# A mixture-of-experts layer behind windowed attention: shared tiles ahead of the expert search, deviations for two pairs at once, routed sums behind the low part

## The chip, the cores and the metric

The kernel runs on one core of one Trainium2 chip. Its time is the device time of one execution in microseconds (us); three runs were taken. The engines are PE (TensorE), DVE (VectorE), ACT (ScalarE), POOL (GpSimd) and SP (SyncE, here a DMA queue).

## The reference, cut to what matters

`x` has 4 x 2048 tokens of 256 channels (8192 tokens, 64 tiles of 128). The layer is two residual steps:

```python
x = x + layernorm(attn(layernorm(x), w_lin))
y = layernorm(x)
x = x + layernorm(ffn(y))

def ffn(y):
    shared = silu(y @ shared_w_gate.T) * (y @ shared_w_up.T) @ shared_w_down.T   # 704 inner columns
    shared = shared * sigmoid(y @ shared_gate_w.T)
    probs = softmax(y @ gate_w.T)                       # 16 experts
    rw, sel = top_k(probs, 2); rw = rw / rw.sum(-1)
    routed = sum over the two chosen experts: rw * (silu(g) * h) @ w_down[e],  g, h = split(y @ w_gate_up[e])
    return routed + shared
```

All products are made of three float32r products (a number is split in a high part, which is what float32r holds of it, and a low part, which is the rest), so every operand of a product is first copied to its high part (by ACT) and then subtracted to its low part (by DVE).

## The kernel before, in words

There are three stages behind the attention stage, which ends at about 391 us. The order of the work of each engine is written out by hand, with semaphores between the engines.

**Shared tiles.** The 8192 tokens are 16 tiles `n` of 512; each is worked in 6 steps `m` over the 704 inner columns (five of 128, a last one of 64). `Shared.products` is PE's order: in each step it makes the gate and up products of two steps ahead (`gate_up`, L788, 12 matmuls; 6 in the last step of a tile), then what `between` puts in, then `down` of this step (L804, 12 matmuls; 8 in the last). ACT makes silu (`silu`, L746) and the high part of the inner product (`inner_high`, L751), DVE the gated product `hf` (`gated`, L768) and its low part (`inner_low`, L774: tile `hl`, in a last step `hh`). PE's `gate_up` of step k+2 waits for `hf` of step k, `down` of step k waits for its low part. ACT's `leave` takes a whole tile's result out of PSUM.

**Routing stage** (`route_and_share`, tiles 0 to 6: 42 steps, k = 6 n + m). DVE first finds the two best experts of the last 8 token tiles (`choose`, which calls `top.find`) and marks both choices for all 64 tiles (`chosen`), and then begins the 42 steps. Behind `inner_low` of its step stands a part of the routing: weights (k = 0), counts (1), bases (2), `before` (3), places (4), slots (5, 6), rows and blocks (6), block columns (7). From step `LIST_FROM` = 8 on, over 26 steps, DVE writes a group of five list entries (`listed`, L1066 and L1067), POOL their other operand (`in_row`, L945), and PE sums them one step later (`take`, L1131, five matmuls). The finished list gives the row numbers of each expert block (`ids`, step 35); POOL gathers the first four blocks with them. Expert weights are loaded on SP's queue, copied by ACT (`COPY_AT`) and lowered by DVE (`LOW_AT`) between the steps. ACT's exponents of the routing (`gap`, `zs`) need the Exp table; they stand ahead of step 0, between two loads of tables. `done` makes DVE wait for its own operation.

**Expert stage** (`experts`): 144 blocks of 128 rows; POOL gathers their rows (L843), the result goes to `expert_rows` in DRAM.

**Closing stage** (`shared_and_combine`, tiles 7 to 15: 54 steps). Beside the shared tiles it finishes all tokens in 32 units of two tiles of 128 tokens. `sums_at` says in which step DVE makes the `sums` of a unit. For each unit POOL gathers four times 128 expert rows (`gather`, L1380, tile `cy`), DVE adds both routed rows, weighted, to the shared result `ff`, and takes mean and variance (`sums`, L1438 to L1450; eight operations), POOL makes one over the deviation (`scales`, L1387 an add, L1389 a power with exponent -0.5), ACT centres `ff` one step behind the sums (`centred`, L1402), and DVE multiplies and adds `x` (`finish`, L1486), `finish_at` = four steps behind the sums. SP stores the unit. POOL's queue is `scales` of a unit, then the gathers of four units later (`AHEAD` = 4). The last two units need the last tile of the shared part: `routed_sums` (L1457, L1461) prepare them in steps 3 and 4 of tile 15, ahead of DVE's next gated product; `last_sums` (L1471 to L1478) add the shared part when PE is done, and `finish` of the last two ends the kernel. In between, units 28 and 29 are finished ahead of `last_sums`.

Of the kernel before, what the change touches and what calls it, by code (L numbers as in the profile page):

```python
# [12 lines left out]
ALU = mybir.AluOpType  # L13
ACT = mybir.ActivationFunctionType
# [696 lines left out]
CHUNKS = T // 512  # L711
# [135 lines left out]
GROUP = 5  # L847
LISTS = NT * TOPK
GROUPS = -(-LISTS // GROUP)
LIST_FROM = 8  # L850
COPY_AT = {4 + 2 * e: e for e in range(13)} | {36: 13, 38: 14, 40: 15}
LOW_AT = {5 + 2 * e: e for e in range(13)} | {37: 13, 39: 14, 41: 15}
LOAD_AT = {2 * e: e for e in range(15)} | {38: 15}
# [2 lines left out]
def route_and_share(nc, block, sh, sems, we, split, parts, eh, el, xg, xg_in, turned, ynt_d, yn_d, logits, slots, share, shgate, ids,  # L856
# [4 lines left out]
    with ExitStack() as ctx:  # L861
# [88 lines left out]

        @block.scalar
        def _(act):
            act.preload_act_table(ACT.Exp)
            nc.scalar.activation(ones_r[:], ones[:], ACT.Copy)
            act.wait_ge(s["below_ok"], 2)
            nc.scalar.activation(below_r[:], below[:], ACT.Copy).then_inc(s["below_ok"], 1)
            act.wait_ge(s["gap_ok"], 1)
            nc.scalar.activation(gap[:], gap[:], ACT.Exp).then_inc(s["exp_ok"], 1)
            nc.scalar.activation(zs[:], logits[:, :, E], ACT.Exp, scale=-1.0).then_inc(s["exp_ok"], 1)
            act.preload_act_table(ACT.Silu)  # L960

            def leave(n):
                if n > 0:
                    act.wait_ge(s_kept, n * 16)
                sh.leave(act, n, lambda t: (so[:, t:t + 1], s["so_ok"]))

            for n in range(FIRST):
                for m in range(FT):
                    k = n * FT + m
                    sh.silu(act, n, m)  # L970
                    if m == 1 and n > 0:
                        leave(n - 1)
                    sh.inner_high(act, n, m)
                    if m == 2:
                        sh.split_high(act, n + 1)
                    if k in COPY_AT:
                        e = COPY_AT[k]
                        act.wait_ge(s[f"e_in{e % 2}"], e // 2 * 16 + 16)
                        nc.scalar.activation(eh[:, e:e + 1], eraw[:, e % 2:e % 2 + 1], ACT.Copy).then_inc(s["e_hi"], 1)
# [6 lines left out]
        def _(ve):  # L986
# [5 lines left out]
            def choose():  # L992
                top.find(ve, top.EARLY, NT, pick, rest)
                v.tensor_tensor(gap[:], best[:, 1], best[:, 0], ALU.subtract).then_inc(s["gap_ok"], 1)
# [79 lines left out]
                v.tensor_tensor(el[:, e:e + 1], eraw[:, e % 2:e % 2 + 1], eh[:, e:e + 1].bitcast(F32),  # L1074
                                ALU.subtract).then_inc(s["e_lo"], 1)

            choose()
            chosen()
            for n in range(FIRST):
                for m in range(FT):  # L1080
                    k = n * FT + m
                    sh.gated(ve, n, m)
                    if m == 3:
                        sh.split_low(ve, n + 1)
                    if k in LOW_AT and k > 34:
                        expert_low(LOW_AT[k])
                    if k == LIST_FROM + GROUPS + 1:
                        ve.wait_ge(s["taken_ok"], GROUPS)
                        done(v.tensor_copy(ids_f[:], pb[6][:, NBK:2 * NBK]))
                        v.scalar_tensor_tensor(ids[:], pb[6][:, 0:NBK], float(P), ids_f[:], ALU.mult, ALU.add  # L1090
                                               ).then_inc(s["ids_ok"], 1)
                    sh.inner_low(ve, n, m)
                    if k == 0:
                        weights()
                    if k == 1:
                        counts()
                    if k == 2:
                        bases()
                    if k == 3:
                        before()  # L1100
                    if k == 4:
                        places()
                    if k == 5:
                        slots_of(0)
                    if k == 6:
                        slots_of(1)
                        rows_and_blocks()
                    if k == 7:
                        block_columns()
                    if k == 11:  # L1110
                        ve.wait_ge(s["turn_ok"], 1)
                        done(v.tensor_copy(block_expert[:, 0:NBK], pb[7][0:1, 0:NBK]))
                    if k in LOW_AT and k < 34:
                        expert_low(LOW_AT[k])
                    if 0 <= k - LIST_FROM < GROUPS:
                        listed(k - LIST_FROM)

        @block.tensor
        def _(pe):
            hb = both[:].rearrange("p t e -> p (t e)")  # L1120

            def sums(of):
                for k in range(2):
                    nc.tensor.matmul(pb[6 + k][:], of[:], hb[:, 512 * k:512 * k + 512], start=True, stop=True).then_inc(s["sums_ok"], 1)

            def take(g):
                pe.wait_ge(s["listed_ok"], g + 1)
                pe.wait_ge(s["rowed_ok"], g + 1)
                for j in range(g * GROUP, min(g * GROUP + GROUP, LISTS)):
                    w = j % (2 * GROUP)  # L1130
                    ins = nc.tensor.matmul(pb[6][:, 0:2 * NBK], in_row[:, w], in_blk[:, w].rearrange("p v w -> p (v w)"),  # L1131
                                           start=(j == 0), stop=(j == LISTS - 1), skip_group_check=True)
                ins.then_inc(s["taken_ok"], 1)

            def between(n, m):
                k = n * FT + m
                if k == 0:
                    pe.wait_ge(s["below_ok"], 3)
                    pe.wait_ge(s["both_ok"], 1)
                    sums(ones_r)  # L1140
                if k == 2:
                    pe.wait_ge(s["cs_ok"], 1)
                    sums(below_r)
                if k == 9:
                    pe.wait_ge(s["bcol_ok"], 1)
                    for c in range(NBT):
                        ins = nc.tensor.matmul(pb[7][0:1, c * P:(c + 1) * P], bcol[:, c:c + 1], ident[:], start=True, stop=True)
                    ins.then_inc(s["turn_ok"], 1)
                if 0 <= k - LIST_FROM - 1 < GROUPS:
                    take(k - LIST_FROM - 1)  # L1150
                if m == 0 and n > 0:
                    pe.wait_ge(s["so_ok"], n * 4)
                if k == FIRST * FT - 1:
                    pe.sem_inc(x_full, 8)
                    pe.wait_ge(sems["hf_ok"], FIRST * FT - 1)
                    for b in range(2):
                        pe.wait_ge(xg_in[b], 16)
                        for c in range(CC):
                            ins = nc.tensor.transpose(pb[b][:, c * P:(c + 1) * P], xg[:, b, c * P:(c + 1) * P], ident[:])
                        ins.then_inc(x_full, 1)  # L1160
            sh.products(pe, 0, FIRST, between)
# [152 lines left out]
def shared_and_combine(nc, block, sh, yo_out, sems, split, turned, ynt_d, x2_d, yg_d, s_kept, sh_d, neg_half, eps, slots, share, shgate, out, pb):  # L1314
# [13 lines left out]
    UNITS = len(order)  # L1328
    place = {unit: i for i, unit in enumerate(order)}
    steps = [(n, m) for n in range(FIRST, CHUNKS) for m in range(FT)]  # L1330
    finish_at = {steps[k + 4]: sums_at[at] for k, at in enumerate(steps) if at in sums_at and k + 4 < len(steps)}
    centre_at = {steps[k + 1]: sums_at[at] for k, at in enumerate(steps) if at in sums_at and k + 1 < len(steps)}
    with ExitStack() as ctx:
        def sb(name, shape, dt=F32):
# [35 lines left out]
        def _(po):  # L1370
# [12 lines left out]

            def scales(i):
                r = i % R
                po.wait_ge(s["mv_ok"], i * 2 + 2)
                nc.gpsimd.tensor_tensor(rstd[:, r], mv[:, r, :, 1], eps[:, 0:2], ALU.add).then_inc(s["var_ok"], 1)  # L1387
                po.wait_ge(s["var_ok"], i + 1)
                nc.gpsimd.tensor_tensor(rstd[:, r], rstd[:, r], neg_half[:, 0:2], ALU.pow).then_inc(s["dev_ok"], 1)  # L1389
            for i in range(UNITS + AHEAD):  # L1390
                if i >= AHEAD:
                    scales(i - AHEAD)
                if i < UNITS:
                    gather(i)

        @block.scalar
        def _(act):
# [30 lines left out]
        def _(ve):  # L1428
# [60 lines left out]
            for n in range(FIRST, CHUNKS):  # L1489
                for m in range(FT):  # L1490
                    sh.gated(ve, n, m)
                    if m == 1 and n + 1 < CHUNKS:
                        sh.split_low(ve, n + 1)
                    if (n, m) in finish_at:
                        finish(finish_at[n, m])
                    if (n, m) in sums_at:
                        sums(sums_at[n, m])
                    if (n, m) == (FIRST, 0):
                        for k in range(8):
                            ve.wait_ge(yo_out[k], 16 + NBK // 8 * 16)  # L1500
                    sh.inner_low(ve, n, m)
                    if n == CHUNKS - 1 and m in (3, 4):
                        routed_sums(UNITS - 2 + m - 3)
            for i in range(UNITS - 2):
                if i not in finish_at.values():
                    finish(i)
            for i in (UNITS - 2, UNITS - 1):
                last_sums(i)
            for i in (UNITS - 2, UNITS - 1):
                finish(i)  # L1510

# [36 lines left out]
```

## Time and profile before

| | |
|---|---|
| three runs | 1035.18, 1038.87, 1041.07 us (median 1038.87) |
| the profiled execution | 1037.57 us, span of its core 1035.8 us |
| busy | PE 92%, DVE 82%, POOL 56%, ACT 53% of the span |
| instructions | 26916 |

The span is the profiled execution from its first to its last instruction; the execution's own time is 1.8 us longer. PE's load of weights runs beside its matmuls. "issue" is time in which an engine waited for nothing that the profile shows; a releaser is inferred from semaphores. DMA issues on POOL count as its busy time where the row says DMA_INDIRECT.

### The profile page before, as it was taken

The numbers are of one execution on the slowest core, as the hardware profiler recorded it, in microseconds if no ns is written. First come the engines' busy times: TensorE is split into PE (matmuls) and PEld (weight loads), VectorE is DVE, ScalarE is ACT, GpSimd is POOL, SyncE is SP. The second block draws the span as 40 slices with busy tenths as digits, with TensorE's granted clock in tenths as the row PEclk, the third lists the DMA queues.
The fourth block names the chain that finished last, engine by engine and source line by source line (L and its number), as shares of the span: only waits on it lengthen the run. The fifth ranks groups of instructions, "written<-read, shape, count | busy, mean of one in ns | idle before, by whom it ended". The sixth has DMA issues, their size and how long they took to land.

```text
span 1035.8 us, 26916 instructions
## 1 busy us (share of the span) xinstructions
PE 951.2 (92%) x9256; PEld 833.6 (80%) x9256; DVE 844.7 (82%) x2278; ACT 550.8 (53%) x1308; POOL 582.2 (56%) x843
## 2 busy tenths in 40 slices
PE   5997899899789976899999999999999999999994
PEld 4766788687678865788888899999999878788883
DVE  5887998789799868888886588888888678788886
ACT  4995354799434453333434555555555445454542
POOL 4441655622056540268884366666662688888874
PEclk9998999899999988999999999999999999999996
DMA  5532578843268851122232465555556656665653
GB/s 164 172 110 59 163 208 247 259 124 113 65 173 225 236 186 62 50 88 62 76 119 62 88 202 176 179 177 175 176 180 134 188 178 186 190 199 172 207 166 110
DMA packets 155811, 158.17 MB, mean 153 GB/s; under 512 B 52528, under 2 KB 135600, under 8 KB 155696
## 3 DMA queue, kind: packets, MB, share of 16 engines
q1 hardware_dynamic: 137648, 113.98, 35.7%
q0 software_dynamic: 13056, 35.67, 13.0%
q10 hardware_dynamic: 4992, 6.95, 2.2%
q8 instruction: 78, 1.28, 0.5%
q14 instruction: 37, 0.30, 0.1%
HBM read 91.90 MB, written 64.63 MB: 151 GB/s over the span
## 4 chain that ended last, share of the span: by engine, by line
PE 25%; POOL 17%; DVE 12%; issue 4%; ACT 2%; DMA 1%; POOLq 0%; DVEq 0%; SPq 0%; ACTq 0%
POOL cy L1380 14%; PE bank L1245 11%; PE bank L1261 5%; PE bank L788 3%; PE bank L1230 3%; DVE in_blk L1067 2%; POOL crstd L1389 2%; PE bank L804 2%; DVE in_blk L1066 2%; DVE hf L768 2%; DVE hl L774 2%; ACT hh L751 1%; PE bank L1254 1%; DVE el L1074 1%; POOL crstd L1387 1%
## 5 line engine op out<-in xcount | busy, mean ns | idle before, releaser
L843 POOL DMA_INDIRECT xg<-yn_scratch,ids x144 | 137.0, 951 | 94.2 <-PE bank L1230 65.3
L1380 POOL DMA_INDIRECT cy<-expert_rows,slots x128 | 143.4, 1120 | 56.4 <-issue 36.5
L751 ACT ACTIVATE hh<-hf 128x512 fp32r<-128x512 f32 x96 | 60.7, 633 | 202.9 <-DVE hf L768 202.9
L788 PE MATMUL bank<-yh,gh 128*128 128x512 f32 x352 | 141.0, 401 | 12.5 <-DVE hf L768 12.3
L667 PE MATMUL bank<-xbd,am 128*32 128x68 f32 x4096 | 138.3, 304 | 13.6 <-DMA xbd<-xn_scratch 7.9
L667 PEld LDWEIGHTS bank<-xbd,am 128*32 128x32 f32 x4096 | 123.0, 129 | 21.3 <-issue 10.4
L788 PE MATMUL bank<-yh,gl 128*128 128x512 f32 x352 | 140.1, 398 | 0.0
L788 PE MATMUL bank<-yl,gh 128*128 128x512 f32 x352 | 139.2, 395 | 0.0
L945 POOL TENSOR_SCALAR in_row<-col,row_f 128x128 bf16<-128x128 bf16 x128 | 96.6, 771 | 65.6 <-DVE row_f L1051 39.6
L804 PE MATMUL bank<-dh,hh 128*128 128x256 f32 x384 | 110.2, 292 | 11.8 <-DVE hl L774 8.0
L804 PE MATMUL bank<-dl,hh 128*128 128x256 f32 x384 | 106.5, 282 | 0.0
L1245 PE MATMUL bank<-eh,xh 128*128 x288 | 100.4, 348 | 1.6 <-issue 0.6
L804 PE MATMUL bank<-dh,hl 128*128 128x256 f32 x320 | 90.8, 284 | 0.0
L804 PEld LDWEIGHTS bank<-dh,hh 128*128 128x128 f32 x384 | 73.3, 191 | 18.7 <-DVE hl L774 11.0
L788 PEld LDWEIGHTS bank<-yh,gh 128*128 128x128 f32 x352 | 66.8, 190 | 26.0 <-DVE hf L768 12.2
L356 POOL TENSOR_TENSOR rstd<-mv,eps 128x2 f32<-128x2 f32 (+1 forms) x68 | 14.1, 208 | 129.1 <-DVE mv L440 82.5
L450 DVE TENSOR_TENSOR am<-probs,mask 128x512 f32<-128x512 f32 x128 | 80.0, 687 | 8.2 <-ACT probs L545 7.2
L768 DVE TENSOR_TENSOR hf<-sg,bank 128x512 f32<-128x512 f32 x96 | 65.5, 682 | 24.1 <-ACT sg L746 23.2
L382 POOL TENSOR_TENSOR x<-av,xr 128x256 f32<-128x256 f32 x64 | 47.0, 754 | 65.9 <-ACT yn L568 62.5
L1245 PE MATMUL bank<-el,xh 128*128 x288 | 81.2, 282 | 0.0
L1245 PE MATMUL bank<-eh,xl 128*128 x288 | 80.7, 280 | 0.0
L788 PEld LDWEIGHTS bank<-yh,gl 128*128 128x128 f32 x352 | 66.7, 189 | 15.6
(184 smaller groups left out, 2684.2 us busy)
## 6 DMA issues: line engine op xcount, KB each, us to landing
expert_rows<-yo SPq DMA_DIRECT2D x144, 128.0 KB
xbd<-xn_scratch SPq DMA_DIRECT2D x128, 72.0 KB, 2.3
xt<-xp SPq DMA_DIRECT2D x32, 256.0 KB, 2.7
xn_scratch<-xn SPq DMA_DIRECT2D x64, 128.0 KB, 2.7
xr<-x SPq DMA_DIRECT2D x32, 256.0 KB, 3.6
x_scratch<-x SPq DMA_DIRECT2D x32, 256.0 KB, 3.8
yn_scratch<-yn SPq DMA_DIRECT2D x32, 256.0 KB, 3.7
ynt_scratch<-ynt SPq DMA_DIRECT2D x32, 256.0 KB, 4.4
```

Source lines behind the costliest of these rows:

```text
L382: nc.gpsimd.tensor_tensor(x2[:, q, t], av[:, q, t], xr[:, q, t], ALU.add).then_inc(s["x2_ok"], 1)
L450: nc.vector.tensor_tensor(am[:, q, g], probs[:, bass.ds(i * CB, CB), g, None, :].to_broadcast([P, CB, 2, J]), mask[:, None].to_broadcast([ ...
L667: ins = nc.tensor.matmul(pso[q][t][J * b:J * b + J, g * MW:(g + 1) * MW], am[:, q, g, e, side], xbd[:, q, e + side, :, g], start=(g == 0 a ...
L751: self.nc.scalar.activation(self.hh[0:f, g], self.hf[0:f, k], ACT.Copy).then_inc(self.s["hh_ok"], 1)
L768: self.nc.vector.tensor_tensor(self.hf[0:f, k], self.sg[0:f, k], up, ALU.mult).then_inc(self.s["hf_ok"], 1)
L788: ins = self.nc.tensor.matmul(self.pb[2 * k + half][:], w[:, c, col:col + P], y[:, n % 2, c, :], start=(j == 0), stop=(j == 5))
L804: ins = self.nc.tensor.matmul(o, a[:, g, t * P:(t + 1) * P], w[:, m, :], start=(m == 0 and t % 2 == 0 and j == 0), stop=(m == FT - 1 and j ...
L843: return nc.gpsimd.indirect_dma_start(out=to, out_offset=None, in_=yn_d.rearrange("n p c -> (n p) c"), in_offset=bass.IndirectOffsetOnAxis ...
L945: ins = nc.gpsimd.tensor_scalar(in_row[:, w], col[:, 0:P], row_f[:, k, t:t + 1], None, ALU.is_equal)
L1245: ins = nc.tensor.matmul(pg[r % 2][:, 0:2 * MF], a[:, r % 2, c * P:(c + 1) * P], w[:, bass.ds(e, 1), c * C:(c + 1) * C], start=(j == 0), s ...
L1261: ins = nc.tensor.matmul(py[r % 2][:, 0:C], a[:, r % 2], w[:, bass.ds(e, 1), 2 * C:3 * C], start=(j == 0), stop=(j == 2))
L1380: nc.gpsimd.indirect_dma_start(out=y[:, r, t, j], out_offset=None, in_=yg_d, in_offset=bass.IndirectOffsetOnAxis(ap=slots[:, 2 * unit + t, ...
```

## The change

Four edits, all of order and grouping; what is computed stays the same.

1. Routing stage: DVE begins with step 0 of the shared tiles; `choose` stands behind it, `chosen` behind step 1, and the other parts one to three steps later than before. ACT begins with the Silu table; the exponents, between loads of Exp and of Silu, stand in step 3. PE's sums and the turned columns come two steps later.
2. The list is written and taken in steps 10 to 35 instead of 8 to 33; `ids` come in step 37.
3. Closing stage: POOL's `scales` work on two units with one add and one power of four columns, and its loop handles two units: `scales` of a pair, then eight gathers. A unit is finished six steps behind its sums (even) or five (odd).
4. `routed_sums` move from steps 3 and 4 of the last tile to steps 4 and 5, and units 28 and 29 are finished behind `last_sums`.

```diff
-LIST_FROM = 8
+LIST_FROM = 10
...
         @block.scalar
-            act.preload_act_table(ACT.Exp)
+            act.preload_act_table(ACT.Silu)
...
-            act.wait_ge(s["gap_ok"], 1)
-            nc.scalar.activation(gap[:], gap[:], ACT.Exp).then_inc(s["exp_ok"], 1)
-            nc.scalar.activation(zs[:], logits[:, :, E], ACT.Exp, scale=-1.0).then_inc(s["exp_ok"], 1)
-            act.preload_act_table(ACT.Silu)
+            def exponents():
+                act.preload_act_table(ACT.Exp)
+                act.wait_ge(s["gap_ok"], 1)
+                nc.scalar.activation(gap[:], gap[:], ACT.Exp).then_inc(s["exp_ok"], 1)
+                nc.scalar.activation(zs[:], logits[:, :, E], ACT.Exp, scale=-1.0).then_inc(s["exp_ok"], 1)
+                act.preload_act_table(ACT.Silu)
...
                     sh.inner_high(act, n, m)
+                    if k == 3:
+                        exponents()
...
-            choose()
-            chosen()
             for n in range(FIRST):
...
                     sh.inner_low(ve, n, m)
                     if k == 0:
+                        choose()
+                    if k == 1:
+                        chosen()
+                    if k == 3:
+                        counts()
+                    if k == 4:
+                        bases()
                         weights()
-                    if k == 1:
-                        counts()
-                    if k == 2:
-                        bases()
-                    if k == 3:
+                    if k == 5:
                         before()
-                    if k == 4:
+                    if k == 6:
                         places()
-                    if k == 5:
+                    if k == 7:
                         slots_of(0)
-                    if k == 6:
+                    if k == 8:
                         slots_of(1)
+                    if k == 9:
                         rows_and_blocks()
-                    if k == 7:
                         block_columns()
-                    if k == 11:
+                    if k == 13:
...
-                if k == 0:
+                if k == 2:
                     pe.wait_ge(s["below_ok"], 3)
                     pe.wait_ge(s["both_ok"], 1)
                     sums(ones_r)
-                if k == 2:
+                if k == 4:
                     pe.wait_ge(s["cs_ok"], 1)
                     sums(below_r)
-                if k == 9:
+                if k == 11:
...
-    finish_at = {steps[k + 4]: sums_at[at] for k, at in enumerate(steps) if at in sums_at and k + 4 < len(steps)}
+    behind = {at: k + (6 if sums_at[at] % 2 == 0 else 5) for k, at in enumerate(steps) if at in sums_at}
+    finish_at = {steps[k]: [sums_at[at] for at in behind if behind[at] == k] for k in behind.values() if k < len(steps)}
+    finished = [i for units in finish_at.values() for i in units]
...
-                po.wait_ge(s["mv_ok"], i * 2 + 2)
-                nc.gpsimd.tensor_tensor(rstd[:, r], mv[:, r, :, 1], eps[:, 0:2], ALU.add).then_inc(s["var_ok"], 1)
-                po.wait_ge(s["var_ok"], i + 1)
-                nc.gpsimd.tensor_tensor(rstd[:, r], rstd[:, r], neg_half[:, 0:2], ALU.pow).then_inc(s["dev_ok"], 1)
-            for i in range(UNITS + AHEAD):
+                po.wait_ge(s["mv_ok"], i * 2 + 4)
+                nc.gpsimd.tensor_tensor(rstd[:, r:r + 2], mv[:, r:r + 2, :, 1], eps[:].rearrange("p (a b) -> p a b", a=2), ALU.add
+                                        ).then_inc(s["var_ok"], 1)
+                po.wait_ge(s["var_ok"], i // 2 + 1)
+                nc.gpsimd.tensor_tensor(rstd[:, r:r + 2], rstd[:, r:r + 2], neg_half[:].rearrange("p (a b) -> p a b", a=2), ALU.pow
+                                        ).then_inc(s["dev_ok"], 2)
+            for i in range(0, UNITS + AHEAD, 2):
                 if i >= AHEAD:
                     scales(i - AHEAD)
                 if i < UNITS:
                     gather(i)
+                    gather(i + 1)
...
-                    if n == CHUNKS - 1 and m in (3, 4):
-                        routed_sums(UNITS - 2 + m - 3)
-            for i in range(UNITS - 2):
-                if i not in finish_at.values():
-                    finish(i)
+                    if n == CHUNKS - 1 and m in (4, 5):
+                        routed_sums(UNITS - 2 + m - 4)
             for i in (UNITS - 2, UNITS - 1):
                 last_sums(i)
+            for i in range(UNITS - 2):
+                if i not in finished:
+                    finish(i)
             for i in (UNITS - 2, UNITS - 1):
                 finish(i)
```

## Rows read from the trace of the kernel before

**Rows 1.** The page's first part: busy time, share of the span, instructions.

```profile
PE 951.2 (92%) x9256; PEld 833.6 (80%) x9256; DVE 844.7 (82%) x2278; ACT 550.8 (53%) x1308; POOL 582.2 (56%) x843
```

**Rows 2.** Busy time by windows: stretch, length, each engine's busy time (instructions), PE clock, DMA.

```profile
804.00:1020.00 216.00, 208.04 (x1183) 179.69 (x1182) 175.38 (x414) 105.61 (x207) 174.26 (x186) 1.00 0.61 184
1020.00:1036.00 16.00, 3.94 (x18) 3.35 (x16) 9.54 (x26) 2.44 (x5) 3.54 (x7) 0.50 0.26 85
```

**Rows 3.** Waits, 803 to 1036: who <- for whom, us in total, times, longest.

```profile
POOL cy L1380 <- issue: 36.5, 127, 1.2
...
DVE cx L1486 <- issue: 14.6, 11, 3.2
...
PE bank L804 <- DVE hl L774: 8.0, 5, 2.7
...
DVE cff L1457 <- DMA cy<-expert_rows,slots: 3.5, 2, 2.5
```

**Rows 4.** Timeline, closing stage: start, us, what, [idle before it <- releaser].

```profile
806.32 0.94 POOL L1380 DMA_INDIRECT cy<-expert_rows,slots  x1 [19.91 <-DMA expert_rows<-yo]
...
828.27 0.21 POOL L1387 TENSOR_TENSOR crstd<-cmv,eps 128x2 f32<-128x2 f32 x1
...
884.31 0.72 POOL L1389 TENSOR_TENSOR crstd<-crstd,neg_half 128x2 f32<-128x2 f32 x1
...
885.11 0.88 DVE L1486 SCALAR_TENSOR_TENSOR cx<-cff,crstd,cx 128x256 f32<-128x256 f32 x2 [3.18 <-issue]
...
1018.62 0.95 POOL L1380 DMA_INDIRECT cy<-expert_rows,slots  x1 [0.30 <-issue]
```

**Rows 5.** Groups of POOL by shape, whole span: count | busy us, mean ns | idle.

```profile
L1380 POOL DMA_INDIRECT cy<-expert_rows,slots x128 | 143.4, 1120 | 56.4 <-issue 36.5 <-DMA expert_rows<-yo 19.9
...
L359 POOL TENSOR_TENSOR rstd<-rstd,neg_half 128x4 f32<-128x4 f32 x28 | 28.5, 1017 | 2.2
L359 POOL TENSOR_TENSOR rstd<-rstd,neg_half 128x2 f32<-128x2 f32 x40 | 28.4, 711 | 3.1
L1389 POOL TENSOR_TENSOR crstd<-crstd,neg_half 128x2 f32<-128x2 f32 x32 | 23.9, 746 | 2.5
...
L1387 POOL TENSOR_TENSOR crstd<-cmv,eps 128x2 f32<-128x2 f32 x32 | 10.5, 329 | 9.2 <-DVE cmv L1478 8.5
```

**Rows 6.** Timelines of DVE and PE, end of the closing stage.

```profile
1001.78 0.29 DVE L1450 BATCH_NORM_AGGREGATE cmv<-cst 128x2 f32<-128x6 f32 x2
...
1021.82 0.62 DVE L1457 TENSOR_SCALAR cff<-cy,share 128x256 f32<-128x256 f32 x2 [2.48 <-DMA cy<-expert_rows,slots]
...
1030.82 0.88 DVE L1486 SCALAR_TENSOR_TENSOR cx<-cff,crstd,cx 128x256 f32<-128x256 f32 x2
1032.35 0.88 DVE L1486 SCALAR_TENSOR_TENSOR cx<-cff,crstd,cx 128x256 f32<-128x256 f32 x2 [0.64 <-POOL crstd L1389]
...
1019.40 0.39 PE L804 MATMUL bank<-dh,hh 128*128 128x256 f32 x1 [2.66 <-DVE hl L774]
...
1025.38 0.58 PE L804 MATMUL bank<-dh,hh 128*128 128x256 f32 x1 [3.52 <-DVE hh L774]
...
1027.04 0.41 PE L804 MATMUL bank<-dl,hh 128*128 128x256 f32 x1
```

**Rows 7.** Timelines of the routing stage's beginning.

```profile
395.26 1.28 ACT L960 ACT_TABLE_LOAD   x1
396.56 0.60 ACT L746 ACTIVATE sg<-bank 128x512 f32<-128x512 f32 x1
...
399.06 0.79 PE L788 MATMUL bank<-yh,gh 128*128 128x512 f32 x1 [8.10 <-DVE hf L768]
...
438.22 0.37 DVE L1066 TENSOR_SCALAR in_blk<-col,blk_f 128x144 bf16<-128x144 bf16 x1
...
440.36 0.67 DVE L768 TENSOR_TENSOR hf<-sg,bank 128x512 f32<-128x512 f32 x1
...
449.25 0.79 PE L1131 MATMUL bank<-in_blk,in_row 128*128 128x288 bf16 x5
...
455.10 0.67 DVE L768 TENSOR_TENSOR hf<-sg,bank 128x512 f32<-128x512 f32 x1
```

More of the change, by code:

```diff
@@ L1493, in _ @@
                         sh.split_low(ve, n + 1)
-                    if (n, m) in finish_at:
-                        finish(finish_at[n, m])
+                    for i in finish_at.get((n, m), ()):
+                        finish(i)
                     if (n, m) in sums_at:
@@ L1501, in _ @@
                     sh.inner_low(ve, n, m)
-                    if n == CHUNKS - 1 and m in (3, 4):
-                        routed_sums(UNITS - 2 + m - 3)
-            for i in range(UNITS - 2):
-                if i not in finish_at.values():
-                    finish(i)
+                    if n == CHUNKS - 1 and m in (4, 5):
+                        routed_sums(UNITS - 2 + m - 4)
             for i in (UNITS - 2, UNITS - 1):
                 last_sums(i)
+            for i in range(UNITS - 2):
+                if i not in finished:
+                    finish(i)
             for i in (UNITS - 2, UNITS - 1):
```

## The prediction

> **What bounds the kernel now.** I read the page first, then busy time by windows, the waits of each stage, and last the timelines around the edits. The page says PE is busy 92% of the span and POOL 56% [rows 1]. That mean hides three stages: routing (391 to 584 us), experts (584 to 804), closing (804 to the end). The edits touch the first and the last.
>
> In the closing stage PE is busy 208 of 216 us up to 1020, and then 3.94 of 16 us at half the full clock, the lower of its two levels (1.2 GHz) [rows 2]. So PE is the bound there, and what can be won is its idle time. The waits name it: 8.0 us waiting for the low part hl of DVE and 3.5 us for the last low part (hh), 11.5 us in all [rows 3, 6]. DVE is late because it waits itself: 14.6 us ahead of the finishing operation (L1486) and 3.5 us ahead of the routed sums (L1457) for gathered rows [rows 3]. The first is printed as "issue", but a timeline shows what it is: POOL's power for that unit starts at 884.31 and runs 0.72, to 885.03; DVE had been idle 3.18 and starts at 885.11 [rows 4]. Both waits go back to POOL, which from 806.32 to 1019.57 issues without a rest [rows 4]: 32 units, 6.66 us each, hardly faster than PE uses them up. POOL's pace is the hidden bound.
>
> In the routing stage PE sits idle 8.10 us until DVE has found the last top two and marked them, and starts at 399.06 [rows 7]. After that DVE is nearly saturated until the list is written.
>
> **The change, part by part.**
>
> *Deviations for two units at once.* A unit costs POOL four gathers and one block (add, power). A gather is 1.12 busy [rows 5]; with the pause behind it, about 1.425 (the tile's issues have 36.5 us of such pauses [rows 3]): 128 of them are 182.4 us, and 28 blocks of 1.065 (0.329 + 0.746, [rows 5], small pauses, less the pause saved at a gather) are 29.8, together 212.2 against 213.25 measured [rows 4], so these are the right sizes. A doubled block works on four columns instead of two. The attention stage has both widths of the same power: 1.017 us against 0.711 [rows 5], so 0.31 more; the add does not grow. A pair then costs 1.375 instead of 2.13: 0.755 less, and 14 pairs stand ahead of the last gather: 10.6 us less work on POOL.
>
> The edit adds a wait: a block, and the eight gathers queued behind it on POOL, wait for the sums of the pair's second unit, and DVE's next sums wait for those gathers. At the end of the stage this cap binds: the last eight gathers stand behind the sums of unit 27, which end at 1002.07 today [rows 6] and, with the 5.3 us of PE's idle time ahead of it gone (11.5 - 2.66 - 3.52), near 997. Then 1.4 for the block and 8 times 1.425: issue ends at 1009.6, landing 2.2 later (today the last issue ends at 1019.57 and DVE starts at 1021.82, [rows 4, 6]), so 1012. If nothing of the 5.3 goes, 1017.
>
> *Finishing five or six steps behind the sums instead of four.* Between a unit's sums and its finishing now lie at least 20 us instead of 17, while the deviation comes earlier. I take all 14.6 us of DVE's idle time there as gone. Its price: at six of the steps two units are finished at once (0.8 each, two operations as in [rows 6]) between the gated product and the low part. Five of these have sums as well (2.5: two each of four operations, the last of them in [rows 6]): 0.6 + 1.6 + 2.5 + 0.6 = 5.3 us of DVE. A full step of PE takes 4.2 (the 54 steps, some of them shorter, take 1027.5 - 804 less 11.5 and 1.8: 3.9 each). But these five stand between lighter ones, and a low part is due only 2.8 us after its gated product; so nothing, at most 1.1 us each, 5.5.
>
> *Routed sums behind the low part.* Today these two stand ahead of DVE's next gated product while gathers are awaited: PE idles 2.66 before 1019.40 and 3.52 before 1025.38 [rows 6]. Moved one step back, the first stands after PE has all it needs of its step, and the second has nothing of PE behind it. What is late next is the last low part itself: DVE does routed sums (1.33), the gated product, two finishings (1.6) and the low part (0.6), and PE waits some 2.5 us for it. So of 11.5 us idle 2.5 stay. Today's idle also brought the lower clock: the two last groups took 2.27 and 1.9 instead of 1.42 and 0.95 (the last matmul shows 0.41, against 0.28 where the clock is full), 1.8 us; I take that as gone. The last product ends at 1027.45 today [rows 6]: 1027.45 - 9.0 - 1.8 = 1016.7.
>
> *The tail.* Last sums run from there to 1030.82, and DVE ends at 1032.35 + 0.88 = 1033.23 [rows 6]; the span ends 2.6 later, with the store. Now finishing of units 28 and 29 stands behind the last sums (before, it filled the wait for PE), and the deviations of the last two come together. Last sums 3.3, then four finishings 3.3; the paired block (0.38 + 0.08 + 0.82 + 0.31 = 1.6) lies beside the first two. DVE ends at 1016.7 + 6.6 + 0.1 = 1023.4, which is 9.8 earlier. Four stores leave within 3.3 us instead of two: 0.3 more. **Closing stage: 9.5 us gained.** Bounds: 7 less gain if the cap binds (1.5 to 2) and every crowded step costs; 2.5 more if the last wait goes too.
>
> *Shared tiles ahead of the search, list over ten steps.* PE's idle 8.10 falls to about 3.4: a table load from 391.24, two small copies and silu (1.28 + 0.5 + 0.6, [rows 7] for the first and last) give DVE its first product near 393.7 instead of 398.3. But DVE then stands still 2.4 us waiting for that silu, and its work is the same. It has no slack to give: I followed its order and found it the last to be ready at nearly every step up to the list. Today it begins step 12 at 455.10 [rows 7], having written four lists, of 440.36 - 438.22 = 2.14 each. Now two lists (4.28) and one small copy (0.33) come later, and 2.4 plus 0.8 (a silu that stands behind the splitting of the next tile) are lost idle: 455.10 - 4.6 + 3.2 = 453.7. PE begins that step about 1.0 to 1.4 earlier, with two more list products still to do (five matmuls each, begun at 449.25 and shown as 0.79 long [rows 7]; 0.53 until the next product begins). From there both engines run at about 4.6 us per step in either kernel, and the waits at tile changes come out a little larger. Net: +0.3 us, so the 4.7 us that PE starts earlier come back as waits of 0.5 to 2 us for DVE through the steps 2 to 10. PE's restart at the lower clock (3 us of it) is the same in both. Bounds: 2 us gained, if DVE's order leaves more slack than I see; 3 lost.
>
> *Exponents in step 3.* ACT does a table load, two small operations and a load: 1.30 + 0.57 + 1.30 = 3.2 us ahead of the silu of step 4. DVE counts in that time (3.8), so it costs nothing; 1.1 us of cover is left. The row is clear: the load takes 1.28 us and the next operation begins 0.02 behind it [rows 7]. The Trainium skill (ScalarE: Activation LUTs, What ACT_TABLE_LOAD costs) adds a drain of about 1.38 us to each switch, 2.66 in all. By that rule the block would be 5.9 us and the sum 1.7 worse; the trace does not agree, and the row is used.
>
> *List two steps later.* The ids come at step 37, not 35, some 9 us later; the four gathers behind them on POOL are needed in step 41 and were 15 us early. The low part of expert 13 waits for the last list product, which moves it by some 4.5 us; SP's load for expert 15 waits for that, and its copy in step 40 keeps 4 us of slack. Nothing.
>
> **Sum.** -9.5 + 0.3 = -9.2 us. The profiled execution took 1037.57 (span 1035.8), 1.3 below the median 1038.87 of the three runs, which spread over 6 us. From one base 1028.4, from the other 1029.7; I say 1029.0.
>
> **Rivals.**
> (A) Half a gain: the pair wait and the crowded steps take over the place of the waits removed. For it: the cap is real. Against: 3 us of room in front of it. Price: last gathers at 1017 instead of 1012 (2.2 late for the routed sums), 3.3 for three of the five crowded steps, routing +1: gain 3, time about 1035.5.
>
> (B) POOL's gathers stretch. The steady pitch of 1.425 is itself a guess for a denser stage. If it rose by 0.1, the whole 10.6 us would be used up, and every 0.01 beyond that adds 1.28 us, since all 128 are in line. At 1.58, 11% more, the kernel ends 5 to 6 us later than before: about 1044. It decides from 1.53 on. For it: the first sixteen, with less work on DVE beside them, come at (828.27 - 806.32) / 16 = 1.37 [rows 4], the mean is 1.425. Against: those sixteen have no block between them, so gathers need no block to recover in. The Trainium skill (GPSIMD Engine Reference, Specifications) says GpSimd shares its way into SBUF with VectorE, contended by instructions with two SBUF inputs; these are the finishing and sums. DVE's share would go from 81 to some 85%, and by that rule pitch rises slightly; no row isolates it.
>
> (C) The change in the routing stage wins after all: PE keeps 3 of its 4.7 us. Then 1026. Against: DVE has no free time.
>
> (D) The routed sums alone matter and POOL's pace was no bound: gain 3.2, 1035.
>
> **Chances.** Forecast (1024 to 1032) 0.58, C 0.10, A and D together 0.22, B 0.10 (half of it beyond the bound of a change). A measurement of this kernel can tell 0.5%, 5.2 us. Faster by more: 0.75; within: 0.19; slower: 0.06. Range 1023.5 to 1036: from forecast and C's side to A and D; the forecast's own is 1024 to 1032.
>
> **What would show it.** Right: no DVE idle ahead of L1486 but at the very end; POOL's blocks half as many, with a power of about 1.0; last gather issue ended by 1013; PE's idle time in the closing stage at 2 to 4 us, nearly all before the last low product; in the routing stage PE restarting near 394.4, and the stage still ending within 2 us of 584. Wrong: gathers longer than 1.2 us on average; POOL waiting for sums all along the stage; PE idle ahead of the steps with two finishings; a routing stage shorter or longer by over 3 us.

## The result, and the profile after

The changed kernel takes 1030.31 us (median of 19 runs, 1027.1 to 1035.99), the kernel before beside it 1039.76 (19 runs). The ratio is 0.9906, interval 0.9893 to 0.9920: 9.4 us faster. 1029.0 was predicted. One run of e2 (1468.91 us) and one of e4 (1155.79 us) had a mean granted clock of 0.56 and 0.74 and stand in no ratio below.

The page after, busy time by engine [rows 1]:

```profile
PE 949.1 (92%) x9256; PEld 833.5 (81%) x9256; DVE 844.5 (82%) x2278; ACT 552.4 (54%) x1309; POOL 567.4 (55%) x811
```

The shares hardly move; only POOL's 32 fewer instructions show. By windows of the stages (columns as in [rows 2]):

```profile
806.00:1013.00 207.00, 207.00 (x1183) 180.74 (x1182) 171.71 (x408) 105.23 (x206) 158.72 (x155) 1.00 0.62 190
1013.00:1029.00 16.00, 4.13 (x29) 3.63 (x27) 12.70 (x35) 3.35 (x8) 4.12 (x6) 0.66 0.42 138
```

In the closing stage PE is now busy without a gap up to 1013, where it had 8 us of gaps in 216. The waits that were there before the last tile (5.3 us in all) are gone, so the steps with two finishings cost PE nothing. The waits of DVE there, 803 to 1029 [rows 3]:

```profile
DVE cff L1449 <- DMA cx<-x_scratch: 1.9, 2, 1.3
DVE cff L1449 <- DMA cy<-expert_rows,slots: 1.7, 1, 1.7
...
DVE cx L1497 <- issue: 0.2, 1, 0.2
```

The 14.6 us ahead of the finishing are 0.2, and the 3.5 ahead of the routed sums are gone. New is a wait for `cx<-x_scratch`, the load of `x` (and with it of the shared result) for a unit. POOL, at its first block and at its last gather [rows 4]:

```profile
833.78 1.05 POOL L1398 TENSOR_TENSOR crstd<-crstd,neg_half 128x4 f32<-128x4 f32 x1
...
1013.76 0.96 POOL L1388 DMA_INDIRECT cy<-expert_rows,slots  x1 [0.30 <-issue]
```

It issues from 811.14 to 1014.72, 203.6 us for what took 213.25, 9.7 less. The groups [rows 5] and, below them, the end on DVE and PE [rows 6]:

```profile
L1388 POOL DMA_INDIRECT cy<-expert_rows,slots x128 | 139.7, 1091 | 58.3 <-issue 36.7 <-DMA expert_rows<-yo 20.3 <-DVE cff L1454 1.2
...
L1398 POOL TENSOR_TENSOR crstd<-crstd,neg_half 128x4 f32<-128x4 f32 x16 | 18.9, 1178 | 2.6 <-POOL crstd L1395 0.4
```

```profile
1017.75 0.39 PE L804 MATMUL bank<-dh,hh 128*128 128x256 f32 x1 [2.37 <-DVE hh L774]
...
1019.08 0.41 PE L804 MATMUL bank<-dl,hh 128*128 128x256 f32 x1
...
1022.86 1.67 DVE L1497 SCALAR_TENSOR_TENSOR cx<-cff,crstd,cx 128x256 f32<-128x256 f32 x4
1024.69 1.67 DVE L1497 SCALAR_TENSOR_TENSOR cx<-cff,crstd,cx 128x256 f32<-128x256 f32 x4 [0.17 <-issue]
```

One idle time of PE is left, 2.37 us ahead of the last products, which need the last low part. In the routing stage [rows 7]:

```profile
395.23 0.50 PE L788 MATMUL bank<-yh,gh 128*128 128x512 f32 x1 [3.35 <-DVE hf L768]
...
446.41 0.47 PE L788 MATMUL bank<-yh,gh 128*128 128x512 f32 x1 [2.13 <-DVE hf L768]
```

PE restarts 4.75 us earlier, counted from attention's end (390.96 before, 391.88 here), and at 446.41 0.9 are left of it.

All stage lengths below (us) are read from one profile each, the ratios from all runs of the kernel. Routing is from the end of attention's last matmul to the first turned expert rows. Closing is from its first matmul to DVE's end. PE idle is what PE waits for DVE in the closing stage.

| kernel | ratio to before, interval | routing | closing | PE idle |
|---|---|---|---|---|
| before | 1 | 191.6 | 231.4 | 11.5 |
| changed | 0.9906, 0.9893 to 0.9920 | 193.3 | 220.3 | 2.4 |
| e1_closing | 0.9908, 0.9882 to 0.9933 | 193.0 | 219.9 | 2.4 |
| e2_routing | 0.9995, 0.9976 to 1.0014 | 193.1 | 231.1 | 12.2 |
| e3_pairs | 0.9924, 0.9896 to 0.9952 | 191.9 | 221.8 | 3.7 |
| e4_tail | 0.9962, 0.9943 to 0.9982 | 191.7 | 226.8 | 6.4 |
| e5_finish | 0.9975, 0.9949 to 1.0001 | 191.8 | 228.8 | 10.8 |
| e6_pairs_tail | 0.9901, 0.9867 to 0.9935 | 191.7 | 219.3 | 1.5 |
| e7_no_pairs | 0.9944, 0.9918 to 0.9970 | 192.4 | 224.3 | 3.0 |
| e8_extra_power | 0.9976, 0.9948 to 1.0004 | 193.1 | 228.3 | 5.8 |
| e9_late_share | one run, 1027.82 us | 191.1 | 219.9 | 2.4 |
| e10_pairs_tail_late | 0.9892, 0.9870 to 0.9914 | 191.7 | 219.3 | 1.5 |
| e11_one_input | one run, 1023.44 us | 192.2 | 218.6 | 2.8 |

### The profile page after: what moved, and what is told of

Read it like the earlier page. It is cut to its first block, busy times and chain, and to the rows that moved or that the text cites. A ratio compares the mean times of both kernels' runs of the same rounds, so it can differ in the third digit from the quotient of the medians.

```text
span 1029.0 us, 26902 instructions
## 1 busy us (share of the span) xinstructions
PE 949.1 (92%) x9256; PEld 833.5 (81%) x9256; DVE 844.5 (82%) x2278; ACT 552.4 (54%) x1309; POOL 567.4 (55%) x811
## 4 chain that ended last, share of the span: by engine, by line
PE 35%; DVE 19%; ACT 4%; issue 2%; DMA 1%; SPq 0%; DVEq 0%; POOL 0%; POOLq 0%; ACTq 0%
PE bank L1251 11%; PE bank L788 10%; PE bank L804 5%; PE bank L1267 5%; DVE hf L768 3%; PE bank L1236 3%; DVE hl L774 2%; DVE in_blk L1072 2%; ACT hh L751 2%; DVE in_blk L1071 2%; PE bank L1260 1%; DVE cff L1449 1%; DVE cx L1497 1%; DVE cff L1454 1%; DVE el L1079 1%
## 5 line engine op out<-in xcount | busy, mean ns | idle before, releaser
L1388 POOL DMA_INDIRECT cy<-expert_rows,slots x128 | 139.7, 1091 | 58.3 <-issue 36.7
L667 PEld LDWEIGHTS bank<-xbd,am 128*32 128x32 f32 x4096 | 122.8, 129 | 21.9 <-issue 10.6
L1280 ACT ACTIVATE xh<-bank 128x256 fp32r<-128x256 f32 x144 | 55.3, 385 | 43.7 <-PE bank L1236 42.6
```

The source lines that it names most:

```text
L667: ins = nc.tensor.matmul(pso[q][t][J * b:J * b + J, g * MW:(g + 1) * MW], am[:, q, g, e, side], xbd[:, q, e + side, :, g], start=(g == 0 a ...
L1280: nc.scalar.activation(xh[:, r % 2], px[r % 2][:, 0:C], ACT.Copy).then_inc(s["xh_ok"], 1)
L1388: nc.gpsimd.indirect_dma_start(out=y[:, r, t, j], out_offset=None, in_=yg_d, in_offset=bass.IndirectOffsetOnAxis(ap=slots[:, 2 * unit + t, ...
```

## The experiments

**Which half.** e1 has `route_and_share` of before and `shared_and_combine` of the changed kernel, e2 the reverse.

> The routing stage of before with the closing stage of the changed kernel (deviations in pairs, finishing five or six steps behind, routed sums behind the low part). Theory (POOL's pace and the tail were the whole gain, the routing edit gives nothing or takes 1 to 2 us): 9.5 to 11 us faster than before, ratio 0.990 or a little under, PE idle in the closing stage 2 to 4 us. Rival (both halves gain): 5 to 7 us faster only, the rest in the routing stage.

> The routing stage of the changed kernel with the closing stage of before. Theory: the routing stage, counted from its first to its last matmul, is 1 to 2 us longer than before (the profile of the changed kernel showed 1.6), so the whole is the same or 1 to 2 us slower, ratio 1.000 to 1.002. Rival (the earlier start of PE is kept): 3 to 4 us faster, ratio 0.997.

Measured: e1 is as fast as the changed kernel, e2 as before. The closing stage holds the whole gain; e2's interval leaves room for 2.5 us gained or 1.5 lost. The same order gave routing lengths that differ by 1.3 us from trace to trace, so e1's 193.0 says little by itself. Over all traces above, before's order of that stage (before, e1, e3 to e6, e11) has a mean of 192.0, the changed order (changed, e2, e7, e8) 193.0. By these traces it costs about 1.0 us; the two groups overlap only in e1, and the times can't tell so little.

**Which of the three closing edits.** e3 keeps the pairs alone, e4 the end alone, e5 the finishing alone, e6 the pairs and the end. Against the changed kernel, cut to what matters:

```diff
 # e3, e4, e6: finishing as before
-    behind = {at: k + (6 if sums_at[at] % 2 == 0 else 5) ...}
+    behind = {at: k + 4 ...}
 # e3, e5: end as before; units 28 and 29 are finished ahead of last_sums
-                    if n == CHUNKS - 1 and m in (4, 5):
+                    if n == CHUNKS - 1 and m in (3, 4):
 # e4, e5: scales(i) of one unit and a POOL loop over single units, as before
```

> Before with the paired deviations alone: finishing stays four steps behind, routed sums and the last finishings stay where they were. Theory (POOL's pace is the bound of the closing stage): 6 to 8 us faster, ratio 0.993; DVE's idle time ahead of the finishing falls from 16 to some 4 us; PE idle in the stage about 5 us instead of 11.5. Rival (the order at the end is what matters): 0 to 2 us faster.

> Before with the last routed sums one step later, behind the low part, and units 28 and 29 finished behind the last sums; deviations unit by unit. Theory: 3 us faster (2 to 4), since one of the two long waits ahead of the last low parts goes and POOL's last gathers still end at the same time; ratio 0.997. Rival (this edit is the gain): 7 us or more faster.

> Before with the finishing of a unit five or six steps behind its sums instead of four, and nothing else. Theory (POOL's pace is the bound): DVE's idle time ahead of the finishing goes from 16 to some 1 us, yet the time stays within 1.5 us of before, since DVE then waits for gathered rows at its next sums. Rival (the wait of the finishing is itself what costs): 4 to 5 us faster.

> Before with paired deviations and the new order at the end; finishing four steps behind as before. Theory: 8.5 to 9.5 us faster, all but 1 us of the closing stage's gain: the later finishing adds at most 1 us once POOL is fast. Rival (the three edits add up): 3 us or more less than the whole.

Measured in the closing stage: pairs 9.6 us, end 4.6, finishing 2.6; pairs and end together 12.1, all three 11.2 and 11.6 (changed, e1). They overlap: each takes some of the same waits. e3's time came out where expected (7.9 us, 0.9924), its stage 2 us better. By their ratios e4 gained 4.0 us (2 to 4 expected) and e6 10.3 (8.5 to 9.5 expected). e5 gained 2.6, more than the 1.5 that were allowed, with an interval that touches 1. Its trace shows the idle time move, as expected:

```profile
DVE cff L1440 <- DMA cy<-expert_rows,slots: 6.0, 5, 3.5
...
DVE cff L1459 <- DMA cy<-expert_rows,slots: 3.7, 2, 2.7
DVE cff L1440 <- DMA cx<-x_scratch: 1.4, 1, 1.4
DVE cx L1488 <- POOL crstd L1391: 0.6, 1, 0.6
```

The 16.4 us ahead of the finishing are 0.9, and 9.7 stand ahead of the gathered rows instead of 5.0. e6 shows that the later finishing is not needed: without it the stage is 0.6 to 1.0 us shorter, by one trace of it and two with it.

**POOL's time or the grouping.** e7 is the changed kernel with `scales` and POOL's loop of before. e8 is the changed kernel with one more power per pair:

```diff
+                nc.gpsimd.tensor_tensor(extra[:, i // 2]..., mv[:, r:r + 2, :, 1], neg_half[:]..., ALU.pow)
                 po.wait_ge(s["var_ok"], i // 2 + 1)
```

> The changed kernel with the deviations taken back to one unit at a time (two gathers' groups apart), all else as changed. POOL's work ahead of its last gather grows by 10.6 us. Theory: 6 to 8 us slower than the changed kernel, that is 2 to 4 us faster than before; the last gather's issue ends as late as before, counted from the stage's start. Rival (the pairing did nothing): as fast as the changed kernel.

> The changed kernel with one more power of four columns per pair on POOL, written to a tile that nobody reads: 1.1 to 1.2 us more for each of 14 pairs ahead of the last gather, 16 us in all, of which the first 3 or 4 fall into POOL's free time. Theory: the whole gain of the change is given back, 10 to 14 us slower than the changed kernel and 0 to 4 us slower than before. Rival (the doubling matters for its grouping, not for POOL's time): within 2 us of the changed kernel.

Measured: e7's closing stage is 4.0 us longer than the changed kernel's, e8's 8.0 (by the ratios about 4 and 7; e7's interval just touches the changed kernel's, e8's does not). Direction and order are those of the theory: POOL's time is what counts, with the grouping in place or not. DVE waits for gathered rows again ahead of the routed sums, in e7 for 3.2 us (the row below) and in e8 for 3.5:

```profile
DVE cff L1465 <- DMA cy<-expert_rows,slots: 3.2, 1, 3.2
```

The sizes missed the bounds: 6 to 8 and 10 to 14 were expected, and the issue of e7's last gather ends 212.8 us into the stage, where before it was 217.8 and "as late as before" was expected. The groups of e7 and e8 say why in part:

```profile
L1388 POOL DMA_INDIRECT cy<-expert_rows,slots x128 | 136.8, 1069 | 55.3 <-issue 35.6 <-DMA expert_rows<-yo 19.8
```

```profile
L1389 POOL DMA_INDIRECT cy<-expert_rows,slots x128 | 136.1, 1063 | 56.9 <-issue 36.7 <-DMA expert_rows<-yo 19.9 <-DVE cff L1457 0.3
L1398 POOL TENSOR_TENSOR extra<-cmv,neg_half 128x4 f32<-128x4 f32 x16 | 20.1, 1254 | 0.0
```

A gather is not a constant: 1.12 us before, 1.09 changed, 1.07 and 1.06 here, which over 128 gathers is 2.9 us less in e7 than in the changed kernel and 3.6 in e8. The rest is idle time of POOL that its longer blocks fill. From its first gather to its last, the blocks of e7 take 32.9 us against 20.5 in the changed kernel, 12.4 more, but the 2.9 us for which the changed kernel's POOL waits for the pair's sums are gone, and so are 2.1 us of other pauses. That leaves 4.5 us.

**Is it DVE's reading?** e11 is before with the two additions of routed rows and the finishing made of operations that read one tile; it leaves out what its expectation names. The first of the three:

```diff
-scalar_tensor_tensor(ff[:, r, t], y[:, r, t, 0], share[:, k:k + 1, 0], ff[:, r, t], ALU.mult, ALU.add)
+tensor_scalar(ff[:, r, t], y[:, r, t, 0], share[:, k, 0:1], None, ALU.mult)
```

> Before, with three kinds of DVE operation of the closing stage (both additions of routed rows, the finishing) reading one SBUF tile instead of two; left out by this are the shared part, the first routed row and the residual of all units but the last two's sums. Theory (gathers on POOL stretch while DVE reads two SBUF tiles): the mean gather falls from 1.12 us to 1.05 or less, and POOL ends its last gather 7 us or more earlier, counted from its first. Rival (gathers stretch by themselves, by the DMA queue): mean stays within 0.03 of 1.12.

Measured: mean 1.057, just over the bound set of 1.05; POOL's issue ends 202.2 us after its first gather, 11 earlier. But e3 and e5 to e8, whose operations read two tiles, have 1.06 to 1.08, so this does not tell reading two tiles from reading at other moments. It is inconclusive on the cause: the gathers' length moves with DVE's work beside them, and by what part of it stays open. The stage is shorter too, 218.6, but DVE's own work in it fell from 185 to 166 us by the same edit, so this says nothing of POOL.

**Who paces the routing stage.** e9 is the changed kernel with `shares()` (three of the five operations of `weights`) behind step 38; e10 has e6's closing stage and the same move in before's order.

```diff
+                    if k == 38:
+                        shares()
```

> The changed kernel with half of the weights of the routing (three DVE operations, 0.98 us, which only the closing stage reads) moved from step 4 to step 38. Theory (DVE sets the routing stage up to the end of the list in the changed order): that stage, from the last product of attention to the first turned expert rows, is about 1 us shorter than the changed kernel's 192.4 to 193.3. Rival (PE is the bound there and DVE's load does not count): unchanged.

> Before's routing order with the share of the weights moved to step 38, paired deviations, the new order at the end, and finishing four steps behind as before. Theory: closing stage 219 to 220 us from its first matmul to DVE's end, routing stage about 191.7, so 10 to 11 us faster than before and 1 to 2 us faster than the changed kernel, ratio 0.989 to 0.990. Rival (the changed kernel's finishing five or six steps behind is needed): as slow as the changed kernel or slower.

Measured: e9 191.1, 1.3 under the shortest of the changed order, in one trace. PE's wait at step 5 (0.5 in the changed kernel and in e2) is gone, and from step 6 to step 10 PE begins its gate products 1.1 us earlier than in the four traces of the changed order (53.5 us behind attention's end at step 10, against 54.5 in each). That is the 0.98 us of DVE's work moved away: DVE is the bound there. In before's order the move gives nothing (191.7 with it and in e3 to e6). e10 is the fastest measured over several runs, but its interval overlaps the changed kernel's, so "1 to 2 us faster" than that one is not shown by time. The traces, one each, have 1.0 us less in the closing and 1.6 less in the routing stage.

## Why the prediction was right

*POOL as the hidden bound.* Right, by e3, e7 and e8. The work of its blocks shrank by 10.0 us up to the last gather (30.5 to 20.5), 10.6 were worked out. The power took 1.18, not 1.06: it is longer in this stage than in attention, for a reason that no run isolates. That POOL's whole stretch shrank by nearly the same, 9.7, is partly luck: the gathers took 3.7 less, and waits and pauses 4.1 more.

*The added wait of the pair.* It showed (2.9 us on POOL once, ahead of a block) and cost the stage nothing: the last gather's issue ends 1014.72 - 806.1 = 208.6 us into the stage, and the routed sums found their rows. The prediction had 1009.6 - 801.8 = 207.8.

*Finishing later.* DVE's idle time ahead of it went, as said. The step was over-rated all the same: with pairs its rows are ready at four steps too (2.4 us of waits in e6), and it has a price that I missed. SP's queue stores a unit ahead of loading the fifth after it, so a later finishing delays those loads; that is most likely the wait of 1.9 us for `x_scratch`, which e1, e5, e8 and e9 show too and e3, e4, e6 and e10 do not (e7, with the later finishing, shows none either, so the order of the queue is read from the code and not proved by an experiment).

*The end.* PE's last wait is 2.4 us, 2.5 said. The low clock was taken as gone, and was not quite: the last eight matmuls begin at full clock, fall to 0.41 each and take 1.75 us. In e1, with the same order and the same idle time of 2.37, the clock stayed full and they took 1.21, so the 0.95 of the sum was too short even then. DVE ended 6.9 us after the last product, 6.7 said.

*The size of the closing stage.* It is 11.1 us shorter by these traces, from its first matmul to DVE's end, where 9.8 were worked out for that end. PE's idle time fell by 9.1, as said (9.0). Mis-sized is its busy time, which fell by 3.1 (214.2 to 211.0) and not by the 1.8 of the clock. One reason is that a wait costs PE more than the idle time shown. Before, at the first such wait:

```profile
844.49 0.40 PE L788 MATMUL bank<-yh,gl 128*128 128x512 f32 x1
846.77 0.39 PE L804 MATMUL bank<-dh,hh 128*128 128x256 f32 x1 [1.88 <-DVE hl L774]
846.99 0.28 PE L804 MATMUL bank<-dl,hh 128*128 128x256 f32 x1
```

The first two starts are 2.28 apart, where 0.23 is the pace without a wait, and the next two 0.22 apart instead of 0.12: 2.15 us lost for 1.88 shown. For the five waits that went this makes some 1.3 us, the clock at the end made some 1.1 (both estimates, from these rows and the lengths of the last groups), and the rest stays open.

*Routing: +0.3.* Measured about +1.0 (1.6 in the trace of the changed kernel). The waits up to step 10 came where they were put: 0.9, 1.2, 1.3, 0.5, 1.6, 0.3, 0.6, 0.3 and 2.1, all but the first 0.3 for DVE. At step 12 PE was 1.1 us ahead, within the 1.0 to 1.4 said; in e2, e7 and e8, where the clock fell for 3.4 us at the restart after the wait of 2.1, it was 0.4 behind, and the stage was no longer for it. Mis-sized is the rest: "from there both engines run at about 4.6 us per step in either kernel". DVE, with lists to write, was the later one at tile changes: PE waited 0.73, 0.37, 0.41, 0.37 and 0.41 at steps 16 to 28, against 0.34, 0.32 and 0.33 before, 1.3 more in all. That PE would restart at the lower clock in both kernels was wrong for this trace (see the last section), and it made no difference.

*Not from the edits.* The profiled span fell by 6.8 us only, since attention was 0.9 and the expert stage 1.7 us longer in that trace, with the same code. The medians show 9.4. So the near agreement of 9.2 and 9.4 is in part luck: by the traces the closing stage gained 1.6 us more than its term of 9.5 and the routing stage lost 0.7 more than its 0.3, two errors of opposite sign. The times can't tell so little: e1, with the closing stage alone, gained 9.6 us, with an interval of 7 to 12. The choice of the base (1028.4 or 1029.7) was a guess as well.

Of the rivals, (A) fell with PE's waits: none is left ahead of a crowded step or of the routed sums. (D) fell with e3, where the pairs alone gave 7.9 us. (C) fell with e2. (B) was half alive: the gathers' length does move, but here towards shorter ones.

## What to carry to other kernels

An engine busy half of the span can set the pace of a stage: look whether it issues without a rest and who waits "for issue" just as it ends an operation. Where doubling a small operation costs less than doing it twice (here a power of two columns 0.71 us, of four 1.02), do two units in one; then see who waits for the second of them. And where two engines are near their bound, an earlier start of one returns nothing until the other has less to do. Last, a total that comes out right does not prove its terms: measure each term by its stage.

## What the runs showed of the hardware

An idle time of PE of 3.35 us in the same place ended in two ways. In the changed kernel the clock stayed full (twelve matmuls from 395.23 to 398.27). In e2 the granted clock fell to half, the lower level (1.2 GHz), 1.1 us after the restart, and stayed there for 3.4 us:

```profile
391.64 0.50 PE L788 MATMUL bank<-yh,gh 128*128 128x512 f32 x1 [3.35 <-DVE hf L768]
...
392.97 0.63 PE L788 MATMUL bank<-yh,gl 128*128 128x512 f32 x1
```

Those twelve took 4.5 us instead of 3.0, and the stage was as long as in the changed kernel (193.1 and 193.3): PE then waited 0 and 0.8 us for DVE in the next two steps instead of 0.9 and 1.2, so behind DVE the low clock cost nothing.

The issue of a gather on POOL took from 1.06 to 1.12 us on average. Where only DVE's work beside it was changed, it went from 1.12 to 1.08 (e5, another order) and to 1.06 (e11, other operations). Three traces with the same closing stage (changed, e9, e1) have 1.09, 1.10 and 1.10, so a difference of 0.01 means nothing.
